# First layer's attention: one causal product per batch instead of two chunks with a carried state, and a table addition in two parts

## The reference

```
q = silu(x Wq); k = silu(x Wk); v = silu(x Wv)          # [b, n, h, 16]
step over chunks of 128 tokens, with a state S of 16 x 16 per head:
    scores  = einsum('bchd,bshd->bhcs', q, k) * D        # D = exp(ld*(t-s)), 0 for s > t
    o       = scores v + (q S) * q_decay
    S_new   = chunk_decay * S + einsum('bshd,bshe->bhde', k * k_decay, v)
gate = (x Wg1) Wg2;  o = o * sigmoid(gate)
o = o * rsqrt(mean over the 16 channels of a head of o^2 + eps) * w;   y = o Wo
```

## Time and profile before

| | us |
|---|---|
| median of 3 runs (lowest, highest) | 2542.74 (2542.02, 2550.69) |
| span of the profiled execution | 2560.7 |
| first attention: first matmul of batch 0 to its last addition to X | 52.98 to 621.4 |
| busy in the span: PE, DVE, ACT, POOL | 2029.5, 1536.0, 688.8, 1082.5 |

### The profile page before, as it was taken

The page is one execution under the profiler, slowest core; times in us unless marked ns, Lnnn a source line. Parts: engine busy times, 40 slices in busy tenths (PEclk is TensorE's granted clock), DMA queues, the critical chain, the costliest instruction groups (busy, mean ns, idle before and its releaser), DMA issues.

```text
span 2560.7 us, 42609 instructions
## 1 busy us (share of the span) xinstructions
PE 2029.5 (79%) x14552; PEld 1550.7 (61%) x14552; DVE 1536.0 (60%) x3346; ACT 688.8 (27%) x1422; POOL 1082.5 (42%) x936
## 2 busy tenths in 40 slices
PE   6887777785899658887788788668887778877887
PEld 2666665664899636665566566556666566665443
DVE  2566666664655324554354345358886577999676
ACT  2111111111222224544444344301112221322232
POOL 2656666664755412433333324122233322454233
PEclk8988888997999979999899899879999988998887
DMA  6100000000000153434334434000000100000011
GB/s 212 34 13 13 12 8 10 12 13 28 7 10 8 29 89 56 70 54 55 57 55 58 65 42 64 10 9 9 8 8 28 40 15 19 8 12 11 23 37 39
DMA packets 121314, 86.68 MB, mean 34 GB/s; under 512 B 12780, under 2 KB 116316, under 8 KB 120924
## 3 DMA queue, kind: packets, MB, share of 16 engines
q1 hardware_dynamic: 121180, 84.82, 16.8%
HBM read 62.89 MB, written 16.91 MB: 31 GB/s over the span
## 4 chain that ended last, share of the span: by engine, by line
PE 42%; DVE 20%; SPq 14%; issue 13%; POOL 6%; DMA 4%; ACT 2%; DVEq 1%; POOLq 0%; ACTq 0%
PE PS L988 13%; SPq L2178 9%; SPq L2192 4%; DVE xn L507 4%; POOL l_ms L953 3%; DMA QS<-maxT 3%; PE PS L678 2%; PE PS L786 2%; PE PS L741 2%; PE PS L517 2%; PE PS L1849 2%; PE PS L1871 1%; PE PS L1818 1%; DVE st L486 1%; DVE rt_eq L1291 1%
## 5 line engine op out<-in xcount | busy, mean ns | idle before, releaser
L2034 DVE TENSOR_REDUCE negmax<-PS 128x2 f32<-128x512 f32 (+1 forms) x384 | 241.4, 685 | 306.2 <-PE PS L1813 305.5
L507 DVE TENSOR_SCALAR xn<-X,mv,rs 128x256 f32 (+1 forms) x256 | 283.4, 1148 | 20.5 <-POOL rs L500 19.3
L548 POOL TENSOR_TENSOR X<-X,y_sb 128x512 f32 (+1 forms) x128 | 165.5, 1293 | 234.6 <-DVE y_sb L543 229.6
L1965 ACT ACTIVATE pw<-PS 128x512 f32<-128x512 f32 x256 | 140.6, 595 | 284.0 <-PE PS L1850 283.3
L517 PE MATMUL PS<-ident,xn 128*128 128x128 f32 x512 | 88.5, 300 | 160.8 <-DVE xn L507 160.8
L543 DVE TENSOR_TENSOR y_sb<-PS,ga_sb 128x512 f32<-128x512 f32 x96 | 65.5, 682 | 240.6 <-PE PS L1900 71.9
L527 ACT ACTIVATE hT<-PS,modT 128x256 f32<-128x256 f32 x256 | 130.3, 559 | 271.7 <-PE PS L517 270.4
L1849 PE MATMUL PS<-QS,KS 128*128 128x256 bf16 x512 | 106.9, 289 | 110.6 <-DMA QS<-maxT 110.6
L988 PE MATMUL PS<-we_hi,h_parts 128*128 128x512 f32 x512 | 179.8, 412 | 0.0
L498 POOL TENSOR_TENSOR rs<-mv,eps 128x2 f32<-128x2 f32 x128 | 54.5, 426 | 293.0 <-DVE mv L491 292.9
L517 PEld LDWEIGHTS PS<-ident,xn 128*128 128x128 f32 x512 | 62.3, 151 | 187.4 <-DVE xn L507 173.2
(11 more groups left out here) (272 smaller groups left out, 5092.8 us busy)
## 6 DMA issues: line engine op xcount, KB each, us to landing
ga_sb<-ga_dram SPq DMA_DIRECT2D x128, 128.0 KB, 2.9
qk_dram<-qk_parts SPq DMA_DIRECT2D x16, 768.0 KB, 4.2
QS<-qk_dram SPq DMA_DIRECT2D x192, 64.0 KB
KS<-qk_dram SPq DMA_DIRECT2D x192, 64.0 KB
wmod<-in_wmod SPq DMA_DIRECT2D x4, 1536.0 KB, 9.0
l_kmask<-l_kT SPq DMA_DIRECT2D x128, 32.0 KB, 1.9
y_out<-X SPq DMA_DIRECT2D x16, 256.0 KB, 2.2
X<-in_x SPq DMA_DIRECT2D x1, 3072.0 KB, 18.1
```

The lines of the kernel that those rows point to most:

```text
L507: last_ = dve.tensor_scalar(xn[b.par][:, t, :], xb(b)[:, t, :], mv[b.par][:, t, 0:1], rs[b.par][:, t:t + 1], ALU.subtract, ALU.mult)
L548: pool.tensor_tensor(xb(b), xb(b), y_sb[b.par][:, :, :], ALU.add).then_inc(s.x.sem, 1)
L1965: act.activation(to.rearrange("p a n -> p (a n)"), bank(4 + n), ACT.Exp).then_inc(s.prob.sem, 1)
L2034: dve.tensor_reduce(to, src, AX.X, ALU.max, negate=True).then_inc(s.max.sem, 1)
```

## The change

The first attention is rewritten; everything after it stays.

- State, `l_qdec`, `l_kdec`, the second projection of k, `l_kmask` with its DMAs and memsets are gone. The decay table covers 256 queries per head (`l_decay` 128 x 16 x 256).
- Scores come in 16 jobs per batch. A job takes the two heads in 32 rows of `l_kT` (K = 32) against `l_qT`, which now has two copies per row, one with the odd head's rows zeroed and one with the even head's (`l0_side` as the scale of the Silu). Keys 0 to 127 meet all 256 queries of both heads (512 columns), keys 128 to 255 only queries 128 to 255 (256 columns). Four PSUM banks take the jobs in turn, and DVE multiplies each with its decay.
- Values are packed: 32 columns hold two heads, one of them zero, and the two heads' products are summed in one 32-row strip of PSUM, so the output of a batch is 128 x 512 and its transposes are four instead of eight.
- POOL's addition to the table is cut into two parts of 2144 elements, for batch i-1 instead of i, one before and one after the power; the addition to X moves to the start of the next slot. On DVE, `xn` moves from behind the last product to the middle, and statistics and `pick` from the start of a slot to its end.
- PE's order is interleaved: the projections of q, k, v and gate stand between the score jobs.

```diff
+        l0_age = sb("l0_age", [P, T], F32, work)
+        causal = sb("causal", [P, T], F32, work)
+        l0_side = sb("l0_side", [P, 2], F32, work)
+        l0_decay = sb("l0_decay", [P, HEADS, T], F32, work)
...
-        qT, kT = wbuf("l0_qT", [P, KH, T]), wbuf("l0_kT", [P, KH, T], 1)
-        vpad = wbuf("l0_vpad", [P, TT, HEADS, 32])
-        kraw, kdec, g1T, qdec = wbuf("l0_kraw", [P, D], 1), wbuf("l0_kdec_", [P, D]), wbuf("l0_g1T", [HD, T]), wbuf("l0_qdec_", [P, KH, P])
+        qT, kT = wbuf("l0_qT", [P, KH, 2, T]), wbuf("l0_kT", [P, KH, T])
+        vpad = wbuf("l0_vpad", [P, TT, HEADS // 2, 4, HD])
...
-        prob = wbuf("l0_prob", [P, 4, P], 4)
-        oT = sb("l0_oT", [P, 4, TT, P], F32, work)
+        prob_a, prob_b = wbuf("l0_prob_a", [P, 4, 2, T]), wbuf("l0_prob_b", [P, 4, 2, P])
...
+        JOBS = [(m, r, first_) for m in range(KH) for r2 in (0, 2) for first_ in (True, False) for r in (r2, r2 + 1)]
...
+            def scores(b, jobs):
+                for j in jobs:
+                    m, r, first_ = JOBS[j]
+                    if j == 0:
+                        pe.wait_ge(*s.q(b))
+                        pe.wait_ge(*s.k(b))
+                    if j >= 4:
+                        pe.wait_ge(*s.prob(b, j - 3))
+                    elif (b - 1).ok:
+                        pe.wait_ge(*s.prob(b - 1, N_JOBS + j - 3))
+                    rows_ = slice(32 * r, 32 * r + 32)
+                    if first_:
+                        last_ = pe.matmul(bank(3 + j % 4), kT[b.par][rows_, m, 0:P],
+                                          qT[b.par][rows_, m, :, :].rearrange("p a t -> p (a t)"), start=True, stop=True)
+                    else:
+                        last_ = pe.matmul(bank(3 + j % 4)[:, 0:2 * P], kT[b.par][rows_, m, P:T], qT[b.par][rows_, m, :, P:T],
+                                          start=True, stop=True)
+                    last_.then_inc(s.score.sem, 1)
+
...
+            def values(b, m):
+                pe.wait_ge(*s.prob(b, 8 * m + 8))
+                if m == 0:
+                    pe.wait_ge(*s.v(b))
+                    if (b - 1).ok:
+                        pe.wait_ge(*s.oT(b - 1))
+                for kt in range(TT):
+                    for side in range(2):
+                        for r in range(4):
+                            o = PS[32 * r:32 * r + 32, 7, m * T + kt * P:(m + 1) * T]
+                            v_ = vpad[b.par][:, kt, 4 * m + r, 2 * side:2 * side + 2, :].rearrange("p a e -> p (a e)")
+                            p_ = (prob_a, prob_b)[kt][m][:, r, side, :]
+                            last_ = pe.matmul(o, v_, p_, start=kt == 0 and side == 0, stop=kt == 1 and side == 1)
...
-                if i.ok:
-                    project(i)
-                if (i - 2).ok:
-
...
-                    by_token(i - 2)
-                if (i - 1).ok:
-                    c = i - 1
-                    for u in range(8):
-                        if u == 0 and (i - 2).ok:
-                            pe.wait_ge(*s.u(i - 2))
-                        t_scores(c, u)
...
-                    values(c, 6)
-                    values(c, 7)
-                if (i - 2).ok:
-                    if (i - 1).ok:
-                        pe.wait_ge(*s.prob(i - 1))
-                    normed_T(i - 2)
-                if i.ok:
-                    gate_state(i)
+                c, d = i - 1, i - 2
+                if d.ok:
+                    by_token(d, i)
+                if c.ok:
+                    scores(c, range(0, 4))
+                if i.ok:
+                    project_q(i)
+                if c.ok:
+                    scores(c, range(4, 8))
+                if i.ok:
+                    project_k(i)
+                if c.ok:
+                    scores(c, range(8, 12))
+                    values(c, 0)
+                if i.ok:
+                    project_v(i)
+                if c.ok:
+                    scores(c, range(12, 16))
+                if i.ok:
+                    project_g1(i)
                 ahead(ln_transpose, pe, pl, i, 1)
-                if (i - 2).ok:
-                    out(i - 2)
...
+                if d.ok:
+                    normed_T(d, i)
+                if c.ok:
+                    values(c, 1)
+                if i.ok:
+                    project_gate(i)
+                if d.ok:
+                    out(d)
...
+            def decayed(b, jobs):
+                for j in jobs:
...
+            def slot(i):
+                c, d = i - 1, i - 2
+                if d.ok:
...
+                if c.ok:
+                    decayed(c, range(0, 4))
+                if d.ok:
+                    mean_square(d)
+                if c.ok:
+                    decayed(c, range(4, 8))
                 ahead(ln_apply, dve, pl, i, 1)
-                if i.ok:
-                    dve.wait_ge(*s.state_ps(i))
-                    if (i - 2).ok:
-                        dve.wait_ge(*s.pv(i - 2))
-                    dve.tensor_tensor(state[i.par][:, :], bank(2), l0_own[:, :], ALU.mult).then_inc(s.state.sem, 1)
+                if c.ok:
+                    decayed(c, range(8, 12))
+                if d.ok:
+                    norm(d)
+                if c.ok:
+                    decayed(c, range(12, 16))
                 if i.reg is None and i.off == 0:
                     dve.wait_ge(setup["exp"], 1)
-                    dve.tensor_tensor(l0_decay[:, :, :], l0_decay[:, :, :], causal[:, :].unsqueeze(1).broadcast_to([P, HEADS, P]),
+                    dve.tensor_tensor(l0_decay[:, :, :], l0_decay[:, :, :], causal[:, :].unsqueeze(1).broadcast_to([P, HEADS, T]),
                                       ALU.mult).then_inc(setup["decay"], 1)
-                if i.reg is None and i.off in (0, 1):
+                    dve.wait_ge(setup["decay"], 1)
+                ahead(ln_stats, dve, pl, i, 2)
+                if i.ok:
                     pick(i)
-                if (i - 2).ok:
...
-                ahead(ln_rstd, pool, pl, i, 2)
-                if (i - 2).ok:
-                    b = i - 2
-                    pool.wait_ge(*s.u(b))
+            CUT = KH * INTER + 3 * D
+            N_LUT = 2 * KH * INTER + FT * D
+
+            def add_picked(b, part):
+                pool.wait_ge(*s.pick(b))
+                pool.tensor_tensor(lut_w[:, part], lut_w[:, part], l0_pick[:, part], ALU.add).then_inc(s.picked.sem, 1)
+
+            def slot(i):
+                c, d = i - 1, i - 2
+                if (i - 3).ok:
+                    add_to_x(pool, pl, s, i - 3)
+                ahead(ln_rstd, pool, pl, i, 1)
+                if d.ok:
+                    pool.wait_ge(*s.u(d))
...
-                    pool.wait_ge(*s.ms(b))
+                if c.ok:
+                    add_picked(c, slice(0, CUT))
+                if d.ok:
...
-                    pool.wait_ge(*s.q(i))
-                    if (i - 2).ok:
-                        pool.wait_ge(*s.pv(i - 2))
...
-                if i.ok:
-                    pool.wait_ge(*s.pick(i))
-                    pool.tensor_tensor(lut_w[:, :], lut_w[:, :], l0_pick[:, :], ALU.add).then_inc(s.picked.sem, 1)
-                if (i - 2).ok:
-                    add_to_x(pool, pl, s, i - 2)
...
+                if c.ok:
+                    add_picked(c, slice(CUT, N_LUT))
+
+            slots(pool, slot, -1, LOOP0, B + 2)
```

More of the change, by code:

```diff
@@ L154, in layout @@
     out["l0_ld"] = ld
-    out["l0_ld_col"] = np.ascontiguousarray(np.repeat(ld, HD).reshape(KH, P).T)
-    out["l0_ld_row"] = np.repeat(ld, HD)
     out["l0_nw"] = np.ascontiguousarray(a["L0_attn_norm_w"].reshape(KH, P).T)
-    age = k[None, :] - k[:, None]
+    age = np.arange(T)[None, :] - k[:, None]
     out["l0_age"] = np.maximum(age, 0).astype(f)
     out["causal"] = (age >= 0).astype(f)
[L161 to L166, removed]
+    out["l0_side"] = (k[:, None] // HD % 2 == np.arange(2)[None, :]).astype(f)
+    age = age[:, 0:P]
     pad = np.zeros((FT * P - INTER, D), np.int32)
@@ L231, in build @@
         per_phase = {
[L232 to L235, removed]
+            "L0_attn": {"q_ps": 1, "k_ps": 1, "v_ps": 1, "q": 1, "k": 1, "v": 1, "kg": 1,
+                        "gate_ps": 1, "gate": 1, "score": 16, "prob": 16, "pv": 2, "oT": 1,
+                        "otok_ps": 1, "u": 1, "sq": 1, "ms": 1, "rn_raw": 1, "rn": 1, "og": 1, "ogT_ps": 1, "ogT": 1,
+                        "y_ps": 1, "pick": 1, "picked": 2},
             "L0_ffn": {"gate_ps": FT - 1, "gate": FT, "hid": FT, "hid_hi": FT, "hid_lo": FT, "h_hi": 1, "h_lo": 1, "y_ps": 1},
@@ L667, in l0a_tensor, with project_T, project_q, project_k @@
             pe.wait_ge(setup["pads"], 1)
[L669 to L670 removed]
+            def project_T(b, n, bk, done):
+                for m in range(KH):
+                    for kh in range(KH):
+                        last_ = pe.matmul(bank(bk)[:, m * T:(m + 1) * T], l0_w[n][:, kh, m * P:(m + 1) * P],
```

(18 more changed lines are left out.)

263 lines of the change are left out of this document (83 added, 180 removed).

## The result

The changed kernel takes 2456.94 us (median of 4 runs, 2450.61 to 2460.82), the kernel before 2542.38 (2538.57 to 2550.69): ratio 0.9648, 95% interval 0.9607 to 0.9688. Forecast were 2423 us in a range of 2368 to 2485. The profiled execution has a span of 2448.7. Some executions of a kernel on this chip are slow for a reason that no edit here explains (over 1.5% above its fastest one), and the medians further down leave them out.

A forecast was written before the change was run, and what follows sets the result against it. No engine is full, so the order of waits bounds the kernel. 14 slots from 34.22 to 26.4 us give 109.5, plus 16 at the start, less 6 in the drain: 119.5, hence 2423 us, range 2368 to 2485.

The forecast's parts named there:

- rival B: POOL's power holds DVE's xn as the addition does: 3.2 us more a slot, 2468 us; chance 0.15 with no-real-gain rival.
- The cause of the old slot: DVE's xn stands some 9 us of each 34.22 us slot while POOL adds to the table, and PE with it.
- The power does not hold DVE, the addition does: xn on DVE, reached at about 8.4 us, meets only POOL's power and takes about 0.74 us for two.
- l_og behind the second part, at about 5.3: l_og on DVE comes second to POOL's second part, stands until 18.4 us and is done at 19.1.
- Rival A: l_og passes before POOL's second part; PE sets the slot: 2410 us, or 2368 with row groups side by side; chance 0.14.
- The step that failed: the tail at the upper clock: PE's work after l_og at the slot's end: values 1.6, gate product 0.9, output 1.9 us.
- POOL's chain: Square, first part, power, second part, then l_og, values and output set the slot of 26.4 us.
- PE's sum: PE's work in a slot: 23.7 us, about 25 with pauses, including 10.4 for score jobs; less than 26.4 but close.
- lower bound of 5.2: All PE score jobs of a slot, if 32-row groups overlap two by two; the forecast took 10.4 us instead.
- The 18.5 that the prediction gives PE: PE's sum in a slot by the Trainium skill's row-group rule; the forecast would stay, because POOL's chain sets it.
- Rival D: PE at the lower clock all through: its 25 us become about 47, time about 2715 us; chance 0.06.
- Start and drain: l_u of batch 0 near 91 instead of 106.8 us, gain 16; drain slot 24.5 instead of 18.55, loss 6.

The follow-up runs named there:

- The kernel before with `xn` early: Kernel before the change, with only xn of the next batch moved from behind the eighth product to after the fifth: 2440.62 us, ratio 0.9581.
- the two fillers: Unread matmuls on PE: seven before l_og's transposes, added to the changed kernel, 2446.29 us; three behind the output, added to `l_og` first, 2365.57 us.
- `l_og` first: Changed kernel plus one wait: POOL waits for l_og before starting the second part of the table addition; 2377.37 us, ratio 0.9340.
- the jobs one by one: Changed kernel, but each score job waits until the one before has been written: 2691.43 us, ratio 1.0581.

## Why the prediction was right, and where it was off

**The range held by some luck.** 2457 lies outside the prediction's own 2400 to 2450, and the slot of 28.87 outside its 25 to 28. It lies in 2368 to 2485 because the range took in rival B at 2468, and B did not happen.

**The cause of the old slot: right.** The kernel before with `xn` early removes it alone and gives 8.1 us a slot. Part of that is the clock again: it was low for 105 us before, behind a pause of 6.1 us in each slot, and is low for 5 with the edit.

**The power does not hold DVE, the addition does: right.** `xn` takes 0.73 beside a power of 5.44, so rival B fell. The Trainium skill (SBUF — State Buffer, Who interferes with whom) has DVE in its two-port modes contend with GpSimd, whoever issues first holding the shared ports for its whole instruction. The traces agree for `xn` behind the additions (9.73 and 3.48 us), and with 3.36 for 1.27 us also in the other direction; they do not for the power. That `xn` would meet only the power was not quite right: DVE reached it 7.0 us into the slot, not 8.4, and in twelve slots it waited for the end of the first part, at no cost.

**l_og behind the second part, at about 5.3: right**, 5.18, and done 19.1 us after `y_sb`, as forecast. Rival A did not happen, but its time could be had for one wait.

**The step that failed: the tail at the upper clock.** The sum put values 1.6, gate 0.9 and output 1.9, 4.4 us in all, and POOL's chain as the bound. The chain and its links are as forecast. The tail is 4.50 at the upper clock and 8.52 at the lower. The two slots without the drop took 25.8, four with a short one 27.4 to 27.6, and eight took 29.4 to 30.8. Against 26.4 that is 2.47 a slot, 34.6 in all.

**Why: PE's sum.** I took 10.4 us for the score jobs, in series, and 23.7 for PE, "close to 26.4". Measured are 1.6 us for four jobs, 6.2 in all, near the lower bound of 5.2. So PE was done 3.7 us before `l_og` came, not just in time. The Trainium skill (TensorE: Matmul & The Clock Gate, Part 3: Packing small matmuls) has products in different row groups run concurrently. The trace agrees, for two at a time: the jobs of a pair start 13 ns apart or less. (The 18.5 that the prediction gives PE by the Trainium skill is the 23.7 with the jobs halved to the lower bound; the factor of 3.07 would have made it 16.7.) I wrote that the forecast would stay since POOL sets it. That was the error: less work on an engine that isn't the bound lengthened its pause, the clock fell, and PE's work behind the pause became dearer. Rival D had the price of the lower clock, but only for PE being slow throughout, and against it I had set pauses of "about 1.5 us twice a slot"; measured is one of 3.0 to 3.7 and two of about 1. A clock that falls in each slot's pause was no case of mine, though the 0.90 of the old slot already showed one. The two slots of 25.8, the two fillers and the last column of the table show that pause and clock go together. They don't settle what lowers it: with `l_og` first it fell behind some pauses of 1 to 1.9 us and not behind others. Nor is it settled why it stays low for 3.4 us in one slot and for 20.5 in another.

**Start and drain.** `l_u` of batch 0 comes at 81.83 instead of 91, 9 better. I put that down to the overlap of the jobs too (with the jobs one by one it comes at 105.4, waits and clock included); no run tests it alone. The drain slot is 25.9 instead of 24.5. 34.6 - 9.2 + 1.4 gives 26.8 us of the 34 between 2423 and 2457. The other 7 are the difference of two larger terms, neither of them predicted: the rest of the program is 19.4 us shorter in the profile after, and the distance between profile and median, which I had taken as constant, went from 18 above the median to 8 below it, a shift of 26.

**What the change was worth, by parts.** From 2542 the move of `xn` alone reaches 2441, where PE bounds. The new attention with `l_og` first reaches 2377, with slots of 22.6. As written it lands at 2457, because its second part stands in front of `l_og`.

## What to carry to other kernels

Before moving or splitting a long GpSimd operation, list which DVE instruction issues next to it: here `l_og`, with two SBUF operands, and `xn`, a TENSOR_SCALAR on SBUF, stood for the rest of the addition, while `l_prob`, which reads one operand from PSUM, and the reduction to `l_ms` took their usual 0.7 beside it. One wait that lets the short DVE instruction through first was worth 80 us. An engine made faster off the bound gets longer pauses; price what stands behind the pause at the lower clock too, and where PE pauses in every slot, look at the granted clock before counting the slot.

## What the runs showed of the hardware

- Score jobs in different 32-row groups overlap in pairs, by the records even where a job of the first row group was issued between them: starts 295.636 and 295.649.
- A job that waits for the end of the one before costs 1.18 us for two instructions of 512 columns, against 1.13 for two such jobs side by side, both at the upper clock.
- The power of 5.44 us on 32 elements a partition leaves DVE alone; additions of 4.7 and 9.2 us hold `xn` and `l_og` to their end; `pick` on DVE holds POOL's addition to X for 2.1 us.
- Where PE stood still for 3.0 to 3.7 us in a slot (12 of 14), the granted clock fell around the end of the pause, for 3.4 to 20.5 us; where it stayed low through the tail, the work behind the pause took 8.5 instead of 4.5 us. Where PE did not stand still (2 of 14) it did not fall.
